# Router chain and slot tables of the first expert step in another order, in a graph, attention and mixture-of-experts block on one core

## The reference

```python
xn = xf * rsqrt(mean(xf * xf) + eps)
probs = softmax(xn @ router_w.T)                 # 8 experts
topk_p, topk_i = top_k(probs, 2)
mask = one_hot(topk_i, 8).sum(1)
dispatch = argsort(~mask.T, stable=True)[:, :97] # at most 97 tokens for each expert
xg = xf[dispatch]
eout = (silu(xg @ rg) * (xg @ ru)) @ rd          # each expert, inner width 4096
routed = zeros.at[dispatch].add(eout * weight)
shared = (silu(x @ sg) * (x @ su)) @ sd          # all tokens, inner width 8192
```

## Time and profile before

| what | value |
|---|---|
| median of 3 runs | 2879.48 us (2877.33 to 2880.08) |
| the profiled execution, its own time | 2881.12 us |
| its span, first to last instruction | 2879.4 us |
| mean granted TensorE clock, as a share of full speed | 0.996 |
| PE busy | 2850.3 us, 99% |
| DVE busy | 2233.0 us, 78% |
| ACT busy | 1490.6 us, 52% |
| POOL busy | 56.8 us, 2% |

### The profile page before, as it was taken

How to read it: one execution, slowest core, us unless ns; L and a number is a source line. 1 busy time by engine, 2 the same in 40 slices (tenths; PEclk the granted TensorE clock), 3 DMA queues, 4 the chain that set the end, 5 groups by cost and what they waited for, 6 DMA issues and landing times.

```text
span 2879.4 us, 43193 instructions
## 1 busy us (share of the span) xinstructions
PE 2850.3 (99%) x16150; PEld 2404.8 (84%) x16150; DVE 2233.0 (78%) x2728; ACT 1490.6 (52%) x1941; POOL 56.8 (2%) x73
## 2 busy tenths in 40 slices
PE   9999999999999999999999999999999999999999
PEld 8997899878888888888888888888888888888877
DVE  8745334888888888888888888888888888888888
ACT  7622121555555555555555555555555555555563
POOL 0100000000000000000000000000000000000001
PEclk9999999999999999999999999999999999999999
DMA  3110111366666666666666666666666666666676
GB/s 112 38 59 30 59 59 45 97 227 219 218 228 219 219 217 229 219 219 220 231 220 219 219 224 221 218 218 225 219 219 219 225 223 220 219 226 221 218 259 232
DMA packets 266188, 549.21 MB, mean 191 GB/s; under 512 B 16681, under 2 KB 82473, under 8 KB 265831
## 3 DMA queue, kind: packets, MB, share of 16 engines
q1 hardware_dynamic: 261858, 532.11, 54.2%
q0 software_dynamic: 3936, 14.06, 1.5%
q10 hardware_dynamic: 162, 0.08, 0.0%
HBM read 537.49 MB, written 8.70 MB: 190 GB/s over the span
## 4 chain that ended last, share of the span: by engine, by line
PE 94%; DVE 5%; ACT 0%; issue 0%; DMA 0%; DVEq 0%; SPq 0%; ACTq 0%
PE ps L1877 26%; PE ps L1881 26%; PE ps L1880 26%; PE ps L1614 3%; PE ps L1670 2%; PE ps L1671 2%; PE ps L1669 2%; PE ps L1729 2%; DVE c_lo L1401 2%; PE ps L1654 1%; PE ps L1928 1%; PE ps L1767 1%; PE ps L1765 1%; PE ps L1766 1%; PE ps L1777 0%
## 5 line engine op out<-in xcount | busy, mean ns | idle before, releaser
L1401 DVE TENSOR_TENSOR c_lo<-raw,c_hi 128x1024 fp32r<-128x1024 f32 x832 | 985.4, 1220 | 102.7 <-ACT c_hi L786 102.3
L786 ACT CAST c_hi<-raw 128x1024 fp32r<-128x1024 f32 x832 | 862.9, 1050 | 169.2 <-PE ps L1881 154.2
L1877 PE MATMUL ps<-tok_hi,c_hi 128*128 128x314 f32 x1792 | 552.9, 309 | 0.4 <-ACT ps L804 0.3
L1880 PE MATMUL ps<-tok_lo,c_hi 128*128 128x314 f32 x1792 | 552.1, 308 | 0.0
L1881 PE MATMUL ps<-tok_hi,c_lo 128*128 128x314 f32 x1792 | 552.0, 308 | 0.0
L1877 PE MATMUL ps<-c_hi,xgT_hi 128*97 128x512 f32 x1024 | 404.1, 395 | 2.9 <-DVE xgT_lo L1460 2.9
L1881 PE MATMUL ps<-c_hi,xgT_lo 128*97 128x512 f32 x1024 | 403.9, 394 | 0.0
L1880 PE MATMUL ps<-c_lo,xgT_hi 128*97 128x512 f32 x1024 | 403.0, 394 | 0.0
L1467 DVE TENSOR_TENSOR resid<-ps,resid 125x512 f32<-125x512 f32 x320 | 219.1, 687 | 178.2 <-PE ps L1881 178.1
L1877 PEld LDWEIGHTS ps<-tok_hi,c_hi 128*128 128x128 f32 x1792 | 339.6, 190 | 3.0 <-issue 0.8
L1880 PEld LDWEIGHTS ps<-tok_lo,c_hi 128*128 128x128 f32 x1792 | 339.9, 190 | 1.4
(11 more groups left out here) (253 smaller groups left out, 3960.7 us busy)
## 6 DMA issues: line engine op xcount, KB each, us to landing
raw<-in_L_ffn_rg SPq DMA_DIRECT2D x256, 512.0 KB, 4.7
raw<-in_L_ffn_ru SPq DMA_DIRECT2D x256, 512.0 KB, 4.7
raw<-in_L_ffn_rd SPq DMA_DIRECT2D x256, 512.0 KB, 6.3
raw<-in_L_ffn_sg SPq DMA_DIRECT2D x64, 512.0 KB, 5.2
raw<-in_L_ffn_su SPq DMA_DIRECT2D x64, 512.0 KB, 5.3
raw<-in_L_ffn_sd SPq DMA_DIRECT2D x64, 512.0 KB, 5.6
wl<-in_L_mix_w_qkv SPq DMA_DIRECT2D x6, 2048.0 KB, 7.8
wl<-in_L_gnn_W SPq DMA_DIRECT2D x2, 2048.0 KB, 21.4
```

The costliest lines, as they stand in the source:

```text
L786: nc.scalar.copy(c_hi[u % RING][:], raw_at_(q, r)[:]).then_inc(sem("hi_done"), 1 + (U - UNITS) * (u == UNITS - 1))
L1401: V.tensor_tensor(c_lo[u % RING][:], raw_at_(q, r)[:], c_hi[u % RING][:].bitcast(F32), ALU.subtract).then_inc(sem("lo_done"), 1 + (U - UNI ...
L1877: m = MM(out_, l_hi, r_hi, start=first, stop=False, skip_group_check=skip)
L1880: MM(out_, l_hi, r_lo, start=False, stop=False, skip_group_check=skip)
```

## The change

All of it concerns the end of the preparation and the first expert step.

1. Block preparation: DVE writes its share of `T1` for tile 3 ahead of the low part of `B11`; ACT copies tile 3 ahead of the high part of `B21`.
2. ACT copies the logits out ahead of `keep_e7(0)`, casts units 5 and 6 ahead of `keep_e7(1)`, and does the exp directly behind that, ahead of the two seeds `TO_C`.
3. DVE's `choose` is split. Its first part goes ahead of units 5 and 6, the second (`choose_two`) behind them.
4. PE's `ranks` goes between the products `F_A22` and `F_S4` of half 0, `slot_tokens` for expert 0 directly behind the last product. DVE's `slots` goes ahead of `shared_inner(0)`, the list of expert 0 ahead of `shared_inner(1)`.
5. `more_slots`, which stood among the `shared_add`, goes among the routed units 14 and 16; the lists are read out in two parts (experts 1 to 3, 4 to 7). The two PE parts stand in the midst of `routed_up(0)` and behind it. `kept` and `choice_row` move from units 17, 19 and 21 to 20, 21 and 22.
6. Both halves of `S` lie in the place of `eout`, and the late lists use another PSUM bank. ACT's unit 13 no longer waits for the tables; POOL clears `eout` after the third list.

```diff
+LATE_TOK_BANK = R0
-    S = [place(f"S{i}", [TP, NT, E // 2, CAP], BF16, at=at) for i, at in enumerate((xgT_at, eout_at))]
+    S = [place(f"S{i}", [TP, NT, E // 2, CAP], BF16, at=at) for i, at in enumerate((eout_at, eout_at))]
...
-        pool.wait_ge(sem("tok_done"), 2)
+        pool.wait_ge(sem("tok_done"), 3)
...
                 copy_y(2)
                 block_hi(B11)
+                copy_y(3)
                 block_hi(B21)
-                copy_y(3)
...
-                keep_e7(0)
                 logits_out(0)
                 logits_out(1)
-                keep_e7(1)
+                keep_e7(0)
                 hi(5)
                 hi(6)
+                keep_e7(1)
+                softmax_exp()
                 seed(0, TO_C)
                 seed(1, TO_C)
                 hi(7)
-                softmax_exp()
...
-                for u in range(9, 13):
+                for u in range(9, 14):
                     hi(u)
-                act.wait_ge(sem("tok_ps"), 2)
-                hi(13)
...
             if t == 2:
                 mean_squares()
+            if t == 3:
                 block_lo(B11)
...
         def more_slots(i):
             if i == 0:
                 dve.wait_ge(sem("y_stored"), 2 * 16 * NT)
+            else:
+                dve.wait_ge(sem("tok_ps"), 2)
...
                 block_lo(T4)
+                choose()
                 lo(5)
                 lo(6)
+                choose_two()
                 lo(7)
-                choose()
+                lo(8)
                 shared_up(0)
+                slots()
                 shared_inner(0)
-                lo(8)
                 shared_up(1)
+                slot_tokens(1, slice(0, 1))
                 shared_inner(1)
-                slots()
-                lo(9)
-                shared_add(0)
-                slot_tokens(1, slice(0, 1))
-                more_slots(0)
-                shared_add(1)
-                shared_add(2)
-                more_slots(1)
-                shared_add(3)
-                shared_add(4)
-                slot_tokens(2, slice(1, E))
-                for n in range(5, 8):
-                    lo(n + 5)
+                for n in range(0, 8):
+                    if n % 2 == 0:
+                        lo(9 + n // 2)
                     shared_add(n)
...
                     lo(u)
-                    if u == 17:
+                    if u == 14:
+                        more_slots(0)
+                    if u == 16:
+                        slot_tokens(2, slice(1, E // 2))
+                        more_slots(1)
+                    if u == 20:
+                        slot_tokens(3, slice(E // 2, E))
                         kept()
-                    if u in (19, 21):
-                        choice_row((u - 19) // 2)
+                    if u > 20:
+                        choice_row(u - 21)
...
-                for j in range(2):
-                    product(j, F_A22)
-                    product(j, F_S4)
+                product(0, F_A22)
                 ranks()
+                product(0, F_S4)
+                product(1, F_A22)
+                product(1, F_S4)
+                pe.wait_ge(sem("S_first"), 1)
+                slot_tokens(True, range(1))
                 pe.wait_ge(sem("sh_ready"), count(e, q, 2, 1 + ONE))
...
                 for n in range(2 * NT):
-                    if n == 2:
-                        pe.wait_ge(sem("S_first"), 1)
-                        slot_tokens(True, range(1))
-                    if n == 7:
-                        pe.wait_ge(sem("S_done"), 2)
-                        slot_tokens(False, range(1, E))
                     if n == 8:
-                        pe.wait_ge(sem("tok_done"), 2)
+                        pe.wait_ge(sem("tok_done"), 1)
                         turn_expert()
                     shared_down(n, (1,) if n < 4 else (0, 1))
                 pe.wait_ge(sem("xgT_ready"), 2)
-                routed_up(0)
+                routed_up(0, (0,))
+                pe.wait_ge(sem("S_done"), 1)
+                slot_tokens(False, range(1, E // 2))
+                routed_up(0, (1,))
+                pe.wait_ge(sem("S_done"), 2)
+                slot_tokens(False, range(E // 2, E))
                 pe.wait_ge(sem("sd_added"), count(e, q, 2 * NT, 2 * NT + ONE))
                 routed_up(1, (0,))
...
                 routed_up(1, (1,))
+                pe.wait_ge(sem("tok_done"), 3)
                 routed_down(0, 2)
```

More of the change, by code:

```diff
@@ L1312, in choose, with choose_two @@
             V.tensor_tensor(T["lg"][:], T["lg"][:], wide(rr["mx"]), ALU.subtract).then_inc(sem("lg_done"), 1)
+        def choose_two():
             dve.wait_ge(sem("pr_done"), 1)
@@ L1353, in slot_tokens @@
             dve.wait_ge(sem("tok_ps"), part)
-            pairs = PS[TOK_BANK][0:CAP, 0:2 * E].rearrange("p (e two) -> p e two", two=2)[:, es, :]
+            pairs = PS[TOK_BANK if part == 1 else LATE_TOK_BANK][0:CAP, 0:2 * E].rearrange("p (e two) -> p e two", two=2)[:, es, :]
             link(V.tensor_copy(slot_tok[:, es], pairs[:, :, 0]))
@@ L1864, in slot_tokens @@
                 for t in range(NT):
-                    m = MM(PS[TOK_BANK][0:CAP, 2 * e:2 * e + 2],
+                    m = MM(PS[TOK_BANK if own else LATE_TOK_BANK][0:CAP, 2 * e:2 * e + 2],
                            S_first[:, t, :] if own else S[e // (E // 2)][:, t, e % (E // 2), :], tok_b[:, t, :],
```

## The result

The changed kernel takes 2871.96 us (median of 19 runs, 2871.02 to 2876.74) against 2879.63 us (19 runs, 2876.28 to 2881.66) for the kernel before on the same chip: a ratio of 0.9976, 95% interval 0.9970 to 0.9982, 7.7 us less. The forecast was 2871.2 us. The profiled execution has a span of 2874.3 us, 5.1 less than that of before; it lies some 4 us above the median span of its kind (2.04 of that is a stop in the last step, put down to "issue" at 2849.19), so stretches of the two traces are compared and not their ends.

The account below looks back on a forecast made before the run. DVE, the narrow engine behind PE's first-step stops, was taken as the bound; 2.4 + 2.8 + 7.0 = 12.2 us removed, less 2.3, 1.3 and 0.3, gives 8.3 won: 2871.2 us, range 2867.5 to 2877.0.

Parts of the forecast that it names:

- Front: Block preparation: 1.3 us from PE's wait for DVE's tile 3 share, plus 1.1 of clock, 2.4 us won.
- what is late next: Block preparation: next late is ACT's copy of tile 3, covered by moving it one cast (1.2 us) forward.
- The clock term: Block preparation: one fewer stop spares part of a later half-clock stretch, 1.1 us, bounds 0 and 1.7.
- Logits, 1.1 + 1.7: Logits: PE's 1.1 us wait goes, and the low-clock stretch behind it, 1.7 us; together 2.8.
- shared part, 7.0: Shared products: waits of 0.9, 1.5 and 2.9 us go, and 1.7 us of low clock; together 7.0.
- the added drain: ACT's table load: skill's rule adds about 1.38 us per switch, making the seed 0.4 us late; prediction followed the trace.
- The new waits: Routed part: PE waits 2.3 us for the first r_h and 1.3 more for the second, as DVE is busy throughout.
- The clock behind the new stops: Routed part: loss from low clock behind the two r_h waits taken as 0, up to 1.7 us kept for the range.
- The rival in which the clock takes its share: Front gives no clock back (-1.1), low stretch follows second new stop (-1.7): 5.5 us won, 2874.0; chance 0.18.
- DVE further behind: DVE's stops only half filled, new waits grow: 4.2 us won, 2875.3 to 2877.0; chance 0.16, late seed included.
- starve at low clock: Routed part: PE waits at each unit, clock stays half: 2881.2 to 2882.9; chance 0.08 with other slower endings.
- the seed wasn't late: Shared products: rival of a late seed, each us past 1.0 slack counting fully; chance 0.16 together with DVE behind.

Follow-up runs that it names:

- e6: Changed kernel with ACT's part of the router in the old order, PE's and DVE's order kept; 2877.3 us, ratio to before 0.9990.
- e2: Changed kernel with DVE's semaphore count-up for the first product moved ahead of the block preparation, directly behind the last normalization; 2871.01 us, ratio to before 0.9970.
- e3: Changed kernel with the two later slot tables back among the shared adds and the late lists among the down products; 2872.17 us, ratio 0.9973.
- e5: Changed kernel with GpSimd's clearing of eout made to wait until VectorE is past the first inner layer; 2871.13 us.
- e4: Changed kernel with the two row picks, 14 DVE instructions, merged into one set of 5; 2870.9 us, ratio to before 0.9969.
- e9: Changed kernel with the edits of e2, e4 and e5, and TensorE's 1.58 us stop among the y turns filled for 0.96 us; 2868.92 us.
- e8: Changed kernel with the edits of e2, e4 and e3 together; 2870.43 us, ratio to before 0.9969.
- e1: Changed kernel with both front edits undone (ACT's last copy and cast, DVE's block preparation); 2875.21 us, ratio to before 0.9983.
- e11: Kernel of e2 with the front edits undone as well; 2874.84 us (one run).
- e12: Changed kernel with the 1.58 us stop among the y turns filled as in e9, count-up stop kept; 2871.29 us (one run).

## Why the prediction was right, and where it was not

**The time.** Forecast 2871.2, measured 2871.96, inside the range and faster by 0.24%. The traces gave 6.7 of the 8.3 us at the end of the step, the medians 7.7 of them (with 5.2 to 8.6 by the interval). That the median comes so near is in part luck. Thirteen of the nineteen runs of the changed kernel lie within 1.3 us of its lowest, and five of the nineteen of the kernel before; lowest to lowest it is 5.3 us. Why more runs fall into the low group after the change isn't shown.

**Front: forecast 2.4, measured 0.6.** (By e6, which has the same front and in whose trace the clock fell earlier, it is 19.04 - 17.09 = 1.95.) The step that failed is "what is late next". It named ACT's copy, which was covered, and not DVE's own `sem_inc`s for the first product, which stand behind the whole block preparation. They are no busy instruction and so in no row; the code has them, and e2 shows them at 2.9 us, 1.4 of stop and 1.5 of half clock. The clock term (1.1 us within 0 and 1.7) failed with it: the low stretch was not spared, it moved from the turns onto the products.

**Logits, 1.1 + 1.7, and shared part, 7.0.** Right in sum and by their signs: all four waits are gone, both low stretches at 1.00, DVE's stops of 3.7 and 2.0 us filled. From the logits to the first inner turn 7.33 us were gained against 7.2. With the longer wait put back (2.93 for 2.3) the work taken away there was 0.7 to 0.8 us more than reckoned. Undoing ACT's order alone gave 3.46 of it back. The single terms were not run apart beyond that. One part of the sum doesn't hold as a term of its own: the move of the tables was credited with 1.5 + 2.9 + 1.7 us and charged with 2.3 + 1.3 + 0.3, so 2.2 won, and in e3, without the move, nothing is lost. TensorE's stops were priced one by one, where DVE's queue set the place of the second turn.

**The table load.** The exp began at the load's end; ACT in order of time, the changed kernel:

```profile
550.11 1.28 ACT L777 ACT_TABLE_LOAD   x1
551.41 0.24 ACT L777 ACTIVATE rt_pr<-rt_lg 125x40 f32<-125x40 f32 x1
551.55 0.41 ACT L805 COPY ps<-ps 128x314 f32<-128x314 f32 x1
```

The row was right to be taken and not the added drain. The seed left at 551.55, and no product waited for it.

**The new waits.** The first `r_h`: 2.3 forecast, 2.93 measured; e5 shows 0.74 of it as one VectorE line blocked by a GpSimd clearing. Without it the wait is 2.19. The second: 1.3 against 1.25. The ground given, DVE without a gap and TensorE following it, is shown from both sides, by e4 (less work in the queue: one for one) and e3 (the same work elsewhere: next to nothing). That also shows what the prediction did not ask: the move of the later tables is worth nothing as the kernel stands. Whether it is worth more once DVE's queue is shorter stays open (e9 against e8, with half clock in e8).

**The clock behind the new stops.** Taken at 0, with 1.7 kept. In the changed kernel it stayed at 1.00 behind 2.93 and behind 1.25 us. The first of these was luck: behind the same stop of 2.93 us it fell in two of six traces (e1, e2; not in the changed kernel, e6, e11, e12). What was forecast for that case held: the second wait took it up, all but 0.1 us. The rival in which the clock takes its share came true in its front half. "DVE further behind" was seen in its mechanism alone (0.6 us in the first wait); TensorE didn't starve at low clock (clock 1.00 from 550 us on), and the seed wasn't late.

**The range and the signs.** The lower end of the range doesn't follow from its own terms: all of the front's clock (0.6 more) and the second wait hidden (1.3 more) make 10.2 us won, not 12, which would be 2869.3. TensorE's idle time from the first turn of `y` to the second step was to fall from about 10 to 5 us; it fell from 10.1 to 7.8, of which 1.4 is the stop for the count-up.

## What to carry to other kernels

When a stop is taken from in front of a wait, read the waiting engine's own code for what else that wait asks for: semaphores counted up by plain queue entries show in no row of busy time, and cost what stands ahead of them. Where one engine's queue has no gap, the order of work in it only moves the stops; take instructions out, and keep a GpSimd clearing away from its short lines. Judge a few microseconds from a fixed place in the trace to the next, not by whole runs, and look there at which stretch the clock's fall lay on.

## What the runs showed of the hardware

- The granted clock fell to half behind stops of TensorE of 1.12 us (before, at 550 us; not in e6) and 1.13 us (e8; not in e3), behind one of 1.4 us for the count-up in all five traces that have it, behind one of 1.58 us in five of twelve, behind one of 2.94 us before and one of 2.93 in two of the six traces that have it, and not behind 1.48 us (before, at 577.61) or 1.25 (changed kernel). A fall lasted some 3 to 7 us and cost 0.1 to 1.8 us, by what lay under it. What decides is open; the length of one stop alone doesn't.
- A VectorE `TENSOR_SCALAR` of 125 x 40 took 0.92 instead of 0.18 us while GpSimd cleared 97 x 1024, and ended with it. Two-input `TENSOR_TENSOR`s beside such clearings kept their usual time: `r_h` 0.69 us in e6 (at 601.63, clearing at 601.17) and 0.68 in e9 (604.79, 604.96), four low parts in a row 4.62 us with a clearing among them (changed kernel, at 600.72) and without one (at 588.35).
